# Latent attention: row maxima of the own key group gathered over banks of several heads, with the causal masks of the four diagonal tiles added by TensorE

## The reference, cut to what matters

```
q = apply_rope((x @ Wq.T) per head)
k = apply_rope((latent @ Wuk.T) per head);  v = (latent @ Wuv.T) per head
scores = einsum('bhqd,bhkd->bhqk', q, k) / sqrt(8)
scores = where(causal, scores, -inf)
attn = softmax(scores, axis=-1)
out = einsum('bhqk,bhkd->bhqd', attn, v)
```

## Time and profile before

| | |
|---|---|
| median of three runs | 1738.9 us |
| profiled execution, its time and its span | 1726.56 us and 1725.3 us |
| TensorE, VectorE, ScalarE, GpSimd busy | 1228.5, 1195.7, 946.8, 568.1 us |
| first pass of the block (units 0 to 15 and what drains) | about 494 to 935 us |
| second pass of the block | about 1186 to 1640 us |
| VectorE's reductions of 512 keys (line 1761) | 768, busy 479.7 us |
| VectorE's masked reductions (line 1766) | 512, busy 230.1 us, and 512 accumulator reads, 42.2 us |

### The profile page before, as it was taken

The page is one execution under the profiler, slowest core; times in us unless marked ns, Lnnn a source line. Parts: engine busy times, 40 slices in busy tenths (PEclk is TensorE's granted clock), DMA queues, the critical chain, the costliest instruction groups (busy, mean ns, idle before and its releaser), DMA issues. The chain is left out here.

```text
span 1725.3 us, 36353 instructions
## 1 busy us (share of the span) xinstructions
PE 1228.5 (71%) x13313; PEld 627.6 (36%) x13313; DVE 1195.7 (69%) x3279; ACT 946.8 (55%) x1500; POOL 568.1 (33%) x1032
## 2 busy tenths in 40 slices
PE   2655563457767788999887373876778898988846
PEld 2653453446532222223223273653212222222346
DVE  4358598525767899997873255476789999786335
ACT  1226775112344688888887241144557788888522
POOL 2431177046753331221114233375332111111323
PEclk9987666568557999999998696756799999999869
DMA  9410000021002100000000082000000000000012
GB/s 250 99 48 1 2 3 3 14 69 56 1 1 72 35 2 2 1 2 4 2 2 13 27 212 60 3 1 1 2 1 2 1 1 2 2 2 1 14 46 81
DMA packets 59137, 49.01 MB, mean 28 GB/s; under 512 B 7105, under 2 KB 54194, under 8 KB 58610
## 3 DMA queue, kind: packets, MB, share of 16 engines
q1 hardware_dynamic: 53282, 35.84, 7.9%
q0 software_dynamic: 4736, 9.74, 1.7%
q10 hardware_dynamic: 944, 1.10, 0.2%
HBM read 32.72 MB, written 18.38 MB: 30 GB/s over the span
## 5 line engine op out<-in xcount | busy, mean ns | idle before, releaser
L1709 ACT ACTIVATE arena<-psum 128x1024 f32<-128x1024 f32 (+3 forms) x640 | 560.8, 897 | 185.2 <-PE psum L1602 174.3
L1761 DVE TENSOR_REDUCE arena<-psum 128x1 f32<-128x512 f32 x768 | 479.7, 683 | 63.7 <-PE psum L1592 59.9
L1618 PE MATMUL psum<-arena 128*9 128x256 f32 (+2 forms) x4352 | 346.7, 395 | 1.7 <-POOL arena L1826 1.0
L1592 PE MATMUL psum<-arena 64*128 64x512 bf16 (+3 forms) x1280 | 240.6, 372 | 120.5 <-DVE arena L1761 57.9
L1766 DVE CUSTOM_DVE_ANT_0 arena<-psum,wqkv 128x384 bf16<-128x384 f32 (+3 forms) x512 | 230.1, 486 | 80.0 <-PE psum L1592 78.7
L1602 PE MATMUL psum<-arena 64*128 64x512 bf16 (+3 forms) x1280 | 233.4, 362 | 19.6 <-ACT arena L1709 14.7
L1826 POOL TENSOR_SCALAR_AFFINE_SELECT arena<-arena 128x256 f32<-128x256 f32 x256 | 103.1, 406 | 318.1 <-ACT arena L1709 315.5
L1592 PEld LDWEIGHTS psum<-arena 64*128 64x128 bf16 x1280 | 64.0, 94 | 376.9 <-DVE arena L1761 198.7
L1618 PEld LDWEIGHTS psum<-arena 128*9 128x9 f32 x4352 | 67.5, 89 | 174.1 <-issue 131.4
L1804 POOL CAST arena<-arena 128x16 bf16<-128x16 f32 x64 | 16.3, 254 | 326.0 <-DVE arena L1772 323.8
L677 DVE TENSOR_SCALAR small<-psum,YT 128x128 f32<-128x128 f32 x168 | 50.5, 342 | 78.4 <-PE psum L587 77.7
(11 more groups left out here) (353 smaller groups left out, 1950.2 us busy)
## 6 DMA issues: line engine op xcount, KB each, us to landing
arena<-taps SPq DMA_DIRECT2D x8, 1024.0 KB, 11.2
big_w<-in_w SPq DMA_DIRECT2D x2, 2048.0 KB, 21.3
ACCn<-made_rows SPq DMA_DIRECT2D x16, 256.0 KB, 3.6
regions<-sorted_rows SPq DMA_DIRECT2D x5, 741.8 KB, 4.6
sorted_rows<-arena SPq DMA_DIRECT2D x2, 1483.5 KB, 14.6
ACCn<-regions SPq DMA_DIRECT2D x32, 64.5 KB, 1.9
w<-in_w SPq DMA_DIRECT2D x2, 1024.0 KB
ACCn<-sorted_rows SPq DMA_DIRECT2D x6, 258.0 KB, 4.0
```

The lines of the kernel that those rows point to most:

```text
L1592: pe.matmul(psum[:, b, 0:w], plain_q[v % 2][rows, a, i * P:(i + 1) * P], keys[rows, 2 * hq + a, c * GW:c * GW + w], start=True, stop=True) ...
L1618: mm = pe.matmul(psum[32 * hh:32 * hh + 9, O_BANK, lo:hi], values[:, tile_of(v, j), 4 * hq + hh, :], prob[(t + hh // 2) % N_PROB][:, hh % ...
L1709: act.activation(prob[t % N_PROB][:, :, off:GW], both, ACT.Exp, scale=INV_SQRT_HD).then_inc(a_got, 1)
L1761: dve.tensor_reduce(place, bank[:, 0:w], AX.X, ALU.max).then_inc(a_max_got, 1)
```

## The change

The own group's items are laid out anew; those of earlier groups keep their shape but now all come first in their unit.

- Of the four query tiles of a group, each has one **diagonal tile** (128 queries by the 128 keys of the same tile). The diagonal tiles of two query tiles and of two head pairs are gathered: four products of 128 columns fill one bank, for each r. TensorE then adds the masks into the same bank: the stationary operand is a 64-row half of the identity (`pick`), the moving one a 64-row half of the mask (`causal`), repeated four times by its access pattern. The first half covers 4 times 128 columns, the second only 4 times the last 64, since the mask of the lower half is zero to the left. VectorE takes one plain `tensor_reduce` with four results.
- The unmasked keys of the own group: tile 3 has 384 (one bank for each head pair), tile 2 has 256 (both head pairs in one bank), tile 1 has 128 (both in one bank). VectorE reduces them to one or two results.
- A unit has 16g + 12 items in place of 16g + 16. `plan` counts with the new numbers. `tensor_tensor_reduce` and its scratch tiles are gone. `row_max` has one place more for each row and head, and the mask is 128 columns wide, in two copies with the halves of the partitions exchanged, made once by GpSimd.

```diff
-        ITEMS_TO = [4 * n for n in TILES_TO]
+        def pairs_of_items(g):
+            own = GW * g
+            pairs = [((i, a, 2 + c), False, [(i, a, GW * c, GW)]) for i in range(GT) for a in range(2) for c in range(g)]
+            pairs += [((slice(2 * p, 2 * p + 2), slice(0, 2), 0), True,
+                       [(i, a, own + P * i, P) for i in (2 * p, 2 * p + 1) for a in range(2)]) for p in range(2)]
+            pairs += [((3, a, 1), False, [(3, a, own, 3 * P)]) for a in range(2)]
+            pairs += [((i, slice(0, 2), 1), False, [(i, a, own, i * P) for a in range(2)]) for i in (2, 1)]
+            return pairs
+        ITEMS = [pairs_of_items(g) for g, _ in ORDER]
+        N_OF = [2 * len(pairs) for pairs in ITEMS]
+        ITEMS_TO = [sum(N_OF[:v]) for v in range(UNITS + 1)]
...
-                places += [(ITEMS_TO[v] + m - m % 2, "max", (v, m)) for m in range(4 * TILES_OF[v])]
+                places += [(ITEMS_TO[v] + m - m % 2, "max", (v, m)) for m in range(N_OF[v])]
...
-                    pe.matmul(psum[:, b, 0:w], plain_q[v % 2][rows, a, i * P:(i + 1) * P],
-                              keys[rows, 2 * hq + a, c * GW:c * GW + w], start=True, stop=True).then_inc(a_max_put, 1)
+                    bank_free(("max", (v, m + 1)))
+                    at = 0
+                    for i, a, key, w in pieces:
+                        for r in range(2):
+                            rows = slice(SLOT * r, SLOT * r + SLOT)
+                            mm = pe.matmul(psum[:, bank_of(("max", (v, m + r))), at:at + w], plain_q[v % 2][rows, a, i * P:(i + 1) * P],
+                                           keys[rows, 2 * hq + a, key:key + w], start=(at == 0), stop=not masked, skip_group_check=True)
...
+                        at += w
+                    if masked:
+                        for half in range(2):
+                            for r in range(2):
+                                rows, lo = slice(SLOT * r, SLOT * r + SLOT), SLOT * half
+                                own = psum[:, bank_of(("max", (v, m + r))), :].rearrange("p (x k) -> p x k", k=P)[:, :, lo:P]
+                                of_half = causal[(r + half) % 2][rows, lo:P].unsqueeze(1).broadcast_to([SLOT, 4, P - lo])
+                                mm = pe.matmul(own, pick[(r + half) % 2][rows, :], of_half, start=False, stop=True, skip_group_check=True)
...
-                        if part < ORDER[v][0]:
-                            dve.tensor_reduce(place, bank[:, 0:w], AX.X, ALU.max).then_inc(a_max_got, 1)
+                        if part:
+                            rows = bank[:, 0:w * len(pieces)].rearrange("p (a k) -> p a k", k=w) if len(pieces) > 1 else bank[:, 0:w]
                         else:
-                            cuts += 1
-                            if cuts > 2:
-                                dve.wait_ge(a_max_got, dve_base + number[event] - 1)
-                            dve.tensor_tensor_reduce(out=masked[cuts % 2][:, 0:w], in0=bank[:, 0:w], in1=causal[:, GW - w:GW], scale=1.0,
-                                                     scalar=LEAST, op0=ALU.add, op1=ALU.max, accum_out=place).then_inc(a_max_got, 1)
+                            rows = bank.rearrange("p (i a k) -> p i a k", i=2, a=2)
+                        dve.tensor_reduce(place, rows, AX.X, ALU.max).then_inc(a_max_got, 1)
```

More of the change, by code:

```diff
@@ L135, in build @@
         skip_d = wqkv[:, 0:D]
-        causal = wqkv[:, D:3 * D].bitcast(BF16)
+        causal = [wqkv[:, D + 64 * k:D + 64 * k + 64].bitcast(BF16) for k in range(2)]
+        pick = [identb[:, :], wqkv[:, D + 128:D + 192].bitcast(BF16)]
         qk_w, norm_w, ln_gb = sb("qk_w", [P, 2, HD]), sb("norm_w", [P, 2]), sb("ln_gb", [KV, 2])
@@ L1535, in latent_attention @@
             turned = small[:, 4:8, :].rearrange("p a (n d) -> p (a n) d", d=HD)
-            row_max = take(111 * K, 64).rearrange("p (n c) -> p n c", c=4)
-            shift, part_, inv_flat = (take(111 * K + 64 + 16 * k, GT * 4) for k in range(3))
+            row_max = take(98 * K, GT * 4 * 5).rearrange("p (i a r c) -> p i a r c", i=GT, a=2, r=2)
+            shift, part_, inv_flat = (take(111 * K + 16 * k, GT * 4) for k in range(3))
             inv_sum = inv_flat.rearrange("p (i h) -> p i h", i=GT)
@@ L1540, in latent_attention @@
             back, zero = take(111 * K + 112, P + 1), stats[:].rearrange("p i s -> p (i s)")[:, 0:32]
-            masked = [take(98 * K + k * GW // 2, GW // 2, BF16) for k in range(2)]
             k_rev = take(109 * K, GW)
@@ L1634, in attention_pe @@
                 pe.wait_ge(a_cleared, B + 1)
+                pe.wait_ge(l_padded, B + 1)
                 for event in events:
@@ L1639, in attention_pe @@
                     elif kind == "max":
-                        maximum(event)
+                        if x[1] % 2 == 0:
+                            maxima(*x)
                     elif kind == "score":
```

42 lines of the change are left out of this document (22 added, 20 removed).

## The result

The changed kernel takes 1723.5 us (median of 8 runs, 1718.8 to 1729.2) against 1738.6 us of the kernel before (8 runs): ratio 0.9913, 95% interval 0.9895 to 0.9931. It is faster by 0.9%, 15 us, where I had forecast 4 us slower. Two further comparisons on other chips gave 0.9937 (0.992 to 0.9955) and 0.9914 (0.9884 to 0.9943), 9 and 13 us.

The account below looks back on a forecast made before the run. VectorE was taken to bound the rising units, TensorE the falling ones. Per pass +0.3, -3.0, +0.6 and +4.1 made +2.0 us; two passes, +4, put 1738.9 at 1743 us, range 1725 to 1764.

Parts of the forecast that it names:

- units 10 to 15, +0.7 each: Falling units: 0.85 us more TensorE work, four fifths of it paid, 0.7 us longer each, +4.1 us a pass.
- units 2 to 6, -0.6 each: Rising units: no short pairs at bursts and fewer crowded scores, 0.6 us shorter each, -3.0 us a pass.
- VectorE, 0.35 us a unit; accumulator reads at nothing: Own groups: four instructions fewer save 0.35 us a unit, only where VectorE bounds; accumulator reads cost nothing beside.
- Masked pair 0.65 us, TensorE +0.85 a unit: Own groups on TensorE at full clock: a masked pair takes 0.65 us, a unit 0.85 us more, 27 us over 32 units.
- The masks are dear: Rival, chance 0.22: a masked pair takes 0.98 us on TensorE, 0.33 more for each of 64, total 1762 us.
- The count by hand: Pair-by-pair count of TensorE and VectorE steps: unit 8 +0.2 us, unit 5 -0.6 us.
- Units 0 and 1, +0.3: Half-clock units: two masked pairs of 1.1 us each show, `shift` is hidden better, +0.3 us together a pass.
- Units 7 to 9, +0.2 each: Units 7 to 9: unit 8's count of +0.2 us applied to each, +0.6 us a pass.
- my first sign of being wrong: Falling units: the prediction is wrong if they do not lengthen.
- the clock rises sooner: Rival, chance 0.15: masked products fill TensorE's waits in units 1 to 3, saving 3 to 4 us a pass, total 1736 us.
- The sign I had named, a clock of unit 2 above 0.8: Granted clock of unit 2: above 0.8 would speak for the rival that the clock rises sooner.
- VectorE's waits vanish: Rival, chance 0.18: full pairs cover bursts, ten rising units a pass gain about 1 us each, total 1727 us.

Follow-up runs that it names:

- e1: The kernel before, unedited, profiled once more: 1727.4 us.
- e13: The kernel before, with the own group's products issued three times in units 0 to 2: 1.0021 of the kernel before.
- e5: The changed kernel again, unedited, on another chip: 1717.3 us, 0.9937 of the kernel before.
- e18: The changed kernel a third time, unedited: 1714.7 us, 0.9914 of the kernel before.
- e16: The changed kernel with own pairs first, each pair's first product issued three times in units 0 and 1, twice in unit 2: 0.9972 of the kernel before.
- e11: The kernel before, with the own group's products issued twice in units 0 to 3: 1.0013 of the kernel before.
- e6: The kernel before, with the plain unmasked reduction for the own items: 1727.3 us, 0.9999 of the kernel before.
- e3: The changed kernel without its mask products, maxima taken over masked keys too: 1700.7 us, 0.984 of the kernel before.
- e8: The changed kernel with each mask added twice in units 10 to 15 of both passes: 1725.6 us.
- e2: The kernel before in the new order only, own items last with old widths and reduction: 1733.2 us, 1.0027 of the kernel before.
- e7: The changed kernel with own pairs, masked ones first, at the head of each unit: 1714.7 us, 0.992 of the kernel before.
- e12: The changed kernel, list laid out by the old item count, with the fewer pairs of maxima spread over it: 0.9905 of the kernel before.
- e4: The changed kernel with mask products only from unit 4 on: 1713.8 us, 0.9911 of the kernel before.
- e9: The kernel before, with the projection of the fourth query pair moved four items later: 0.9992 of the kernel before.

## Why the clock stays up

VectorE over unit 3, first of the kernel before (e1, from its third reduction on; the accumulator reads overlap and are left out), then of the changed kernel:

```profile
1226.28 0.29 DVE L1766 CUSTOM_DVE_ANT_0 arena<-psum,wqkv 128x128 bf16<-128x128 f32 x1
...
1227.28 1.29 DVE L1761 TENSOR_REDUCE arena<-psum 128x1 f32<-128x512 f32 x2 [0.49 <-PE psum L1592]
...
1229.58 1.29 DVE L1761 TENSOR_REDUCE arena<-psum 128x1 f32<-128x512 f32 x2 [0.49 <-PE psum L1592]
1231.38 0.42 DVE L1766 CUSTOM_DVE_ANT_0 arena<-psum,wqkv 128x256 bf16<-128x256 f32 x1 [0.51 <-PE psum L1592]
...
1232.58 1.29 DVE L1761 TENSOR_REDUCE arena<-psum 128x1 f32<-128x512 f32 x2 [0.42 <-PE psum L1592]
...
1243.04 0.69 DVE L1766 CUSTOM_DVE_ANT_0 arena<-psum,wqkv 128x512 bf16<-128x512 f32 x1 [1.66 <-PE psum L1592]
```

```profile
1218.31 9.71 DVE L1795 TENSOR_REDUCE arena<-psum 128x1 f32<-128x512 f32 x16
...
1228.90 1.29 DVE L1795 TENSOR_REDUCE arena<-psum 128x4 f32<-128x512 f32 x2 [0.39 <-PE psum L1620]
1230.57 2.22 DVE L1795 TENSOR_REDUCE arena<-psum 128x4 f32<-128x512 f32 x4 [0.38 <-PE psum L1620]
1233.12 1.02 DVE L1795 TENSOR_REDUCE arena<-psum 128x1 f32<-128x384 f32 x2 [0.33 <-PE psum L1609]
1234.63 1.29 DVE L1795 TENSOR_REDUCE arena<-psum 128x2 f32<-128x512 f32 x2 [0.48 <-PE psum L1609]
1236.15 0.76 DVE L1795 TENSOR_REDUCE arena<-psum 128x2 f32<-128x256 f32 x2 [0.23 <-PE psum L1609]
```

Before, an own pair stands between any two of the earlier key group, and half the unit's pairs are own pairs. While the clock is half (in these rows until about 1232) VectorE waits about 0.5 us for TensorE at nearly every turn. At full clock it does not: in e13's unit 3 at 1.00 the waits are 0.08 to 0.25 us, beside the 1.66 at the projection. Now sixteen reductions follow one another in 9.71 us, 0.607 each, and the waits at the own pairs come to 1.8 us. The windows of 6 us from unit 2 on, second pass, show TensorE's clock meanwhile; before (e1), then changed:

```profile
1201.00:1207.00 6.00, 5.50 (x52) 1.40 (x48) 3.56 (x13) 2.51 (x5) 2.31 (x8) 0.69 0.00 0
1207.00:1213.00 6.00, 3.31 (x32) 0.80 (x33) 5.72 (x17) 3.35 (x4) 5.07 (x14) 0.88 0.01 3
1213.00:1219.00 6.00, 4.88 (x30) 1.93 (x26) 4.29 (x12) 2.32 (x3) 0.81 (x2) 0.50 0.00 0
...
1225.00:1231.00 6.00, 5.22 (x40) 1.62 (x40) 4.84 (x15) 2.70 (x4) 4.33 (x14) 0.50 0.00 0
1231.00:1237.00 6.00, 4.89 (x51) 1.32 (x48) 4.77 (x15) 3.90 (x7) 3.35 (x9) 0.92 0.00 1
```

```profile
1203.00:1209.00 6.00, 4.59 (x49) 1.41 (x46) 5.14 (x10) 3.75 (x6) 3.80 (x11) 0.98 0.00 0
1209.00:1215.00 6.00, 3.91 (x48) 1.97 (x52) 5.57 (x11) 3.42 (x5) 2.34 (x7) 1.00 0.01 3
1215.00:1221.00 6.00, 3.83 (x51) 1.25 (x44) 5.18 (x12) 1.23 (x3) 2.37 (x8) 1.00 0.00 0
```

Both rise to full speed early in unit 2. In the kernel before TensorE was then busy 3.31 of 6 us, and its clock fell back to half (1.2 GHz) until unit 3 was well on. In the changed one it was busy 3.91 and 3.83 of 6, and the clock stayed. It doesn't always stay: in the first pass of e5 and e18 unit 2 shows 0.68, and takes 23.7 us. That is why the gain of units 1 to 3 differs between passes. Which idle stretch makes the clock fall is only argued from such rows, not shown. "TensorE: Matmul & The Clock Gate" of the Trainium skill (Part 1) ties the throttle to activity; e13 to e16 agree in that the clock of unit 2, where products were added, was 0.78 to 1.00. It doesn't rise surely: in the second pass of e11 and e13 unit 3 has 0.74 and 0.72, less than the 0.84 of e1.

## Why the prediction was wrong

Two steps failed, and one of them nearly cancelled out. By the size of the error the first is "units 10 to 15, +0.7 each": forecast at +8.2 us for both passes, measured at +2.0 (e18) and +3.2 (e5) from the end of unit 9 on. The second is "units 2 to 6, -0.6 each", whose sum came near by luck while its units went to both sides. Unit 1 adds 3 us that I did not expect.

- *VectorE, 0.35 us a unit; accumulator reads at nothing*: the reads right (e6). Unit 8's busy time fell by 0.57 us and unit 5's by 0.52, more than 0.35; in unit 3 at full clock by 0.75.
- *Masked pair 0.65 us, TensorE +0.85 a unit*: right, 0.65 and 0.85. I had split it wrongly: four pairs of 128 take 0.23 and not 0.32, and 0.20 pass from the strided pair to the weighing behind it. In e3 a weighing also comes late behind 128 plain columns (0.15 us after the last pair of them starts, where another pair follows after 0.06), so that is no price of the stride. **The masks are dear** is refuted. "PSUM — Partial Sum Buffer" (Specifications) of the Trainium skill has any output that is not contiguous slow a product significantly; the rows here do not agree, with steps of 0.11 us and means of 287 ns against 284.
- *The count by hand*: unit 8 right (39.65, expected near 39.6), unit 5 only in its sign (30.08, expected 29.6).
- *Units 2 to 6, -0.6 each*: **the step whose mechanism failed.** I counted unit 5, where a third of the pairs are own pairs and the clock is full, and carried its result to units 2 and 3, where half are and the clock is not. From e1 to e18 unit 3 went by -5.1 and -3.1 us, unit 2 by +0.1 and -2.9, unit 4 by +0.5 and -0.1, unit 5 by -0.2 both times, unit 6 by +2.3 and +1.6. That is -7.1 us in both passes (-4.0 in e5) against the forecast -6.0: the number is nearly right, and that is luck. What the count lacked is the clock. I had read it for units 0 to 2 alone, while in the first profile unit 3 was at 0.72 and 0.84 too and unit 4 at 0.89 and 0.94. It is worth 3.3 us to the old unit 3 (e13). Unit 6 goes with it too: it took 39.01 us at 1.00 in e8 and 40.26 at 0.96 in the changed kernel, and the kernel before, whose unit 6 e11 leaves as it was, shows the same step, from 38.9 at 1.00 (e1) to this in the second pass of e11:

```profile
1317.27:1357.56 40.29, 32.67 (x312) 8.39 (x310) 37.23 (x83) 24.93 (x28) 4.50 (x13) 0.92 0.01 2
```

Why it dips in unit 6 is not shown; it also does in e2 and e7, with either order.

- *Units 0 and 1, +0.3*: unit 1 went by -1.2 and -1.9, at a clock of 0.50 to 0.54 in both kernels. All its pairs are own pairs. Packing alone doesn't do it, as e12 shows; the layout of the list takes part, and how is open.
- *Units 7 to 9, +0.2 each*: right for units 8 and 9 (39.45 to 39.65 both); unit 7 is 0.3 us shorter (39.20 to 38.88).
- *Units 10 to 15, +0.7 each*: **the step that failed by most.** I priced TensorE's added products and put what the packing saves in the falling part at nothing. The price is right: the masks cost a unit 0.64 us against 0.66. The saving is not nothing: with the masks left out of both, unit 11 goes from 34.14 to 33.34 us. With them, units 10 to 13 of the second pass went by -0.2, -0.2, -0.9 and -0.9 from e1 to e18, where I had +0.7 each; units that do not lengthen were my first sign of being wrong. Unit 12's 22.68 against an expected 24.3 is partly a shift of the cut, since fewer exponentials lie in it (ScalarE 20.71, now 19.47), so whole stretches say more. Behind unit 13 up to the last weighing e5 and e18 take 2.4 to 4.0 us more a pass than e1, of which about 1.75 are a gap of TensorE (last section) and the rest was not traced.
- *Rivals*: **the clock rises sooner** (0.15) is what happened, but not for its reason: without masks in units 0 to 3 (e3, e4) the gain is there too. I had sized it at 3 to 4 us a pass, packing included. Units 1 to 3 gave 6 to 8 in e18, 5 to 6 in e5. Of e18's 8.2 us in unit 3, 1.5 are the packing at full clock, 1.8 the place of the projection, which unit 4 mostly pays back, and 4.9 the clock. Unit 1 gave 3.0 us at an unchanged clock; unit 2 (2.8 us) isn't separated. The sign I had named, a clock of unit 2 above 0.8, came true in three of six passes; unit 3, full in five of six, is the better one. **VectorE's waits vanish** is true for units 1 to 3 only: unit 8 is idle 3.2 us, more than before.

Left open: why the clock stays in some passes and not in others, why unit 1 is shorter, and the stall below. In units 1 to 3 the same program takes 49.9 to 53.7 us from pass to pass.

## What to carry over

Price what a change saves in every stage, not only in the one where it is meant to save: here, in units 11 to 13, the fuller pairs gave back more than the masks cost. A count by hand in one stage holds for stages with the same mix and the same clock; a stage whose granted clock is between its two levels has to be counted on its own, since the same work there took 20.54 or 23.86 us with the clock. A sum that comes out right may hold units that went to both sides; compare unit by unit. Adding dummy products to hold the clock cost more here than it gave.

## What was not expected of the hardware

TensorE stands still at the end of a pass, in unit 15 or just behind it, and the profile shows nothing that it waits for ("issue"); instructions that come late would look like this, but that is not shown. In the changed kernel on the first chip (timeline of TensorE, first pass), and in e18 on another:

```profile
928.96 0.61 PE L1647 MATMUL psum<-arena 128*9 128x256 f32 x4 [0.53 <-issue]
930.38 1.10 PE L1647 MATMUL psum<-arena 128*9 128x256 f32 x5 [0.82 <-issue]
```

```profile
935.06 1.42 PE L1647 MATMUL psum<-arena 128*9 128x512 f32 x8 [1.76 <-issue]
```

On the first chip VectorE waited 5.85 us there in the first pass. Versions of the changed kernel on other chips mostly show one gap of about 1.75 us, and the kernel before there (before again, e6) none. But where the kernel before itself runs at 1738.6 us (the chip of e9 to e12) versions of it have such gaps too. TensorE in unit 15, second pass, of e9 and of e11:

```profile
1617.94 0.34 PE L1592 MATMUL psum<-arena 64*128 64x384 bf16 x2 [2.66 <-issue]
```
```profile
1628.26 0.50 PE L1593 MATMUL psum<-arena 64*128 64x384 bf16 x2 [4.09 <-issue]
```

And this end of a pass is where the chips differ: e9, nearly the kernel before, has a span of 1735.2 us against 1725.2 of e1, and takes 410.9 and 268.0 us from the end of unit 9 on, where e1 takes 406.9 and 260.6. Unit 15 alone takes 24.6 and 23.1 us in e9 and 18.7 and 18.8 in e1. The stalls are read from the rows; what makes them, and why more so on one chip, wasn't tried.
